# A third shared group of a mixture of experts ahead of its expert stage, in halves between other TensorE work

## The reference

```
x = x + attention(layernorm(x))                    # cumulative K^T V state per head
h = layernorm(x)
scores = softmax(h @ Wg); weights, indices = top_k(scores, 4)
for e in range(32):                                # at most CAP = 2048 pairs per expert
    y[tok] += (silu(h[tok] @ W1[e]) * (h[tok] @ W3[e]) @ W2[e]) * weight
z = silu(h @ Ws1) * (h @ Ws3) @ Ws2                # the shared expert, 256 wide inside
out = x + y + z
```

## Time and profile before

| | us |
|---|---|
| three timed runs, median | 640.11 (639.14 to 641.84) |
| the profiled execution | 639.03 |
| its span, first to last instruction | 637.3 |
| TensorE busy (products) | 581.1 (91%) |
| VectorE busy | 365.5 (57%) |
| ScalarE busy | 393.3 (62%) |
| GpSimd busy | 375.0 (59%) |
| mean granted TensorE clock | 0.973 of full |

### The profile page before, as it was taken

The page is one execution under the profiler, slowest core; times in us unless marked ns, Lnnn a source line. Parts: engine busy times, 40 slices in busy tenths (PEclk is TensorE's granted clock), DMA queues, the critical chain, the costliest instruction groups (busy, mean ns, idle before and its releaser), DMA issues.

```text
span 637.3 us, 16757 instructions
## 1 busy us (share of the span) xinstructions
PE 581.1 (91%) x4081; PEld 420.9 (66%) x4081; DVE 365.5 (57%) x1420; ACT 393.3 (62%) x1306; POOL 375.0 (59%) x425
## 2 busy tenths in 40 slices
PE   4799999999999977699899999999999999997981
PEld 1466766666676654268668888888888888554551
DVE  4589999999999995433223233322333223248686
ACT  2589988989898973216656766676666766410100
POOL 4124778787788786605445555565665555497360
PEclk9999999999999997699999999999999999998995
DMA  8994444444444547957776655565565555397773
GB/s 275 303 291 167 175 169 179 178 161 169 187 161 169 200 185 231 348 173 226 235 224 190 184 181 184 181 186 182 182 182 185 187 180 181 113 412 251 228 264 132
DMA packets 70154, 130.53 MB, mean 205 GB/s; under 512 B 10288, under 2 KB 48560, under 8 KB 70064
## 3 DMA queue, kind: packets, MB, share of 16 engines
q1 hardware_dynamic: 52128, 83.32, 41.1%
q0 software_dynamic: 13824, 41.96, 17.8%
q10 hardware_dynamic: 4112, 4.19, 2.0%
HBM read 61.11 MB, written 68.32 MB: 203 GB/s over the span
## 4 chain that ended last, share of the span: by engine, by line
PE 65%; POOL 10%; issue 8%; DVE 8%; SPq 4%; ACT 3%; DMA 2%; DVEq 0%; ACTq 0%; POOLq 0%
PE pS L730 19%; PE pS L742 9%; PE pS L554 8%; POOL xs L369 6%; PE pQV L659 4%; PE pS L590 3%; POOL w L387 3%; PE pT L723 2%; PE pO L676 2%; PE pQV L723 2%; PE pQV L568 2%; PE pO L568 2%; PE pO L642 1%; DVE xall L994 1%; PE pT L631 1%
## 5 line engine op out<-in xcount | busy, mean ns | idle before, releaser
L398 POOL DMA_INDIRECT ys<-gsh,dst x160 | 152.9, 956 | 131.9 <-ACT gsh L531 130.0
L730 PE MATMUL pS<-w,after_a 128*128 x640 | 165.8, 382 | 0.2 <-ACT after_a L520 0.2
L369 POOL DMA_INDIRECT xs<-xg,posi x128 | 124.3, 971 | 49.6 <-issue 25.6
L730 PEld LDWEIGHTS pS<-w,after_a 128*128 128x128 f32 x640 | 109.1, 190 | 9.8 <-issue 0.6
L742 PE MATMUL pS<-w,after_a 128*128 x320 | 95.6, 381 | 0.0
L1008 DVE COPY after_a<-pO 128x128 f32<-128x128 f32 x80 | 23.3, 292 | 93.0 <-PE pO L737 92.0
L1008 DVE COPY after_a<-pT 128x128 f32<-128x128 f32 x80 | 23.3, 292 | 92.8 <-PE pT L737 91.4
L531 ACT ACTIVATE gsh<-pS,xg 128x256 f32<-128x256 f32 x160 | 75.9, 474 | 0.4 <-issue 0.4
L530 ACT CAST dst<-xg 128x1 int32 x160 | 30.6, 191 | 60.9 <-PE pS L742 60.9
L659 PE MATMUL pQV<-w 128*128 128x512 f32 x128 | 64.0, 624 | 0.5 <-ACT w L464 0.5
L554 PE MATMUL pS<-x2T_all,ws 128*128 128x512 f32 x128 | 62.1, 640 | 2.4 <-DVE gsh L978 1.4
(11 more groups left out here) (157 smaller groups left out, 1105.8 us busy)
## 6 DMA issues: line engine op xcount, KB each, us to landing
xg<-xs SPq DMA_DIRECT2D x160, 160.0 KB, 2.2
ys<-gsh SPq DMA_DIRECT2D x32, 512.0 KB
w<-ys SPq DMA_DIRECT2D x32, 512.0 KB, 6.2
xs<-padrow SPq DMA_DIRECT2D x33, 160.0 KB, 2.4
w<-in_L_ffn_W ACTq DMA_DIRECT2D x1, 4096.0 KB, 21.9
out<-xall SPq DMA_DIRECT2D x32, 128.0 KB, 1.8
xall<-in_L_attn_X SPq DMA_DIRECT2D x1, 3072.0 KB, 14.0
ys<-gsh,dst POOLq DMA_INDIRECT x160, 2.7
```

What stands on the lines that cost most here:

```text
L369: pool.indirect_dma_start(out=xs, out_offset=bass.IndirectOffsetOnAxis(ap=posi[:, a.r8, k:k + 1], axis=0), in_=xr[:, a.r8, :], in_offset=N ...
L398: pool.indirect_dma_start(out=ys, out_offset=bass.IndirectOffsetOnAxis(ap=dst[:, j % 8:j % 8 + 1], axis=0), in_=y[:, j % 8, :], in_offset= ...
L730: last = pe.matmul(pS[a.b][:, 0:2 * F], xgT[:, a.b, k, :], w13[:, bass.ds(e, 1), k, :, :].rearrange("p a n f -> p (a n f)"), start=(k == 0 ...
```

## The change

NPRE becomes 3, so that groups 0, 1 and 2 stand before the experts and 3 to 7 behind them. Eight of the twelve halves go into other banks than `pS[2m+n]`, those that the attention or the table leave free at the time. The halves are issued one at a time between other work: (1,0,0) ahead of tile 27's ranks, (0,0,0) after the last attention output, (0,0,1) and (0,1,0) after the logits of tiles 29 and 30, (0,1,1) between the last transposes and the last logits, (1,0,1) after these, and (1,1,0), (1,1,1), (2,0,0), (2,0,1) after the counts. The row products of the table write into pT0 alone. VectorE does three gates in the middle of the table's chain and the gate of (1,1) behind it, and the last two halves of group 2 stand between the output products.

```
+        early = {(1, 0, 0): pQV, (1, 0, 1): pO, (1, 1, 0): pT1, (1, 1, 1): pS[0], (2, 0, 0): pS[2], (2, 0, 1): pS[1],
+                 (2, 1, 0): pS[3], (2, 1, 1): pT1}
+
+        def h_bank(g, m, n):
+            return early.get((g, m, n), pS[2 * m + n])
-        NPRE = 2
+        NPRE = 3
...
             def shared_half(g, m, n):
-                wait(pe, S["gsh_done"], FC * (g - 1) + m + 1)
                 for k in range(KC):
-                    last = pe.matmul(pS[2 * m + n][:], ws13[:, k, n, m * P:(m + 1) * P],
+                    last = pe.matmul(h_bank(g, m, n)[:], ws13[:, k, n, m * P:(m + 1) * P],
                                      x2T_all[:, k, g * TG:(g + 1) * TG], start=(k == 0), stop=(k == KC - 1))
...
                 if (a := tile_of(6)) is not None:
+                    if a.t == NT - 5:
+                        pe.wait_ge(S["ws_in"], 48)
+                        pe.wait_ge(S["v_done"], NT)
+                        shared_half(1, 0, 0)
...
-            shared_half(0, 1, 1)
+            shared_half(1, 1, 0)
+            pe.wait_ge(S["silu_done"], 1)
+            shared_half(1, 1, 1)
+            pe.wait_ge(S["silu_done"], 2)
+            shared_half(2, 0, 0)
+            pe.wait_ge(S["gsh_done"], 1)
+            shared_half(2, 0, 1)
             pe.wait_ge(S["tab_blk"], 1)
...
-            for g in range(1, NPRE):
-                for m in range(FC):
-                    shared_h(g, m)
-                shared_z(g - 1)
-            shared_z(NPRE - 1)
+            pe.wait_ge(S["gsh_done"], 3)
+            shared_z(0)
+            shared_half(2, 1, 0)
+            shared_z(1)
+            shared_half(2, 1, 1)
+            shared_z(2)
...
+            def half_gate(g, m):
+                wait(dve, S["silu_done"], FC * g + m + 1)
+                wait(dve, S["z_ps"], QT * (g - 1))
+                dve.tensor_tensor(gsh[:, g % 2, m, :], sg[:, m, :], h_bank(g, m, 1)[:], ALU.mult).then_inc(S["gsh_done"], 1)
...
             tab(dve.tensor_tensor_scan(endt[:], ones_f[:], ntf[:], 0.0, ALU.mult, ALU.add))
+            dve.wait_ge(S["ys_zeroed"], 16 * ZC)
+            half_gate(0, 0)
+            half_gate(0, 1)
+            half_gate(1, 0)
...
-            dve.wait_ge(S["ys_zeroed"], 16 * ZC)
-            for g in range(NPRE):
-                shared_gate(g)
-                if g > 0:
-                    shared_add(g - 1)
-            shared_add(NPRE - 1)
+            half_gate(1, 1)
+            shared_add(0)
+            half_gate(2, 0)
+            shared_add(1)
+            half_gate(2, 1)
+            shared_add(2)
```

More of the change, by code:

```diff
@@ L507, in shared_silu @@
                     wait(act, S["gsh_done"], FC * (g - 1) + m + 1)
-                    act.activation(sg[:, m, :], pS[2 * m][:], ACT.Silu).then_inc(S["silu_done"], 1)
+                    act.activation(sg[:, m, :], h_bank(g, m, 0)[:], ACT.Silu).then_inc(S["silu_done"], 1)
             for g in range(NPRE):
@@ L633, in step @@
                     last.then_inc(S["logits_ps"], 1)
+                    if a.t == NT - 3:
+                        shared_half(0, 0, 1)
+                    if a.t == NT - 2:
+                        shared_half(0, 1, 0)
                     if a.t == NT - 1:
-                        shared_half(0, 1, 0)
+                        pe.wait_ge(S["x2_done"], NT)
+                        shared_half(1, 0, 1)
                 if (a := tile_of(2)) is not None:
@@ L685, in _ @@
             pe.matmul(pT0[:, 0:E], ones16[:], mcum[:, NT % 2, :], start=True, stop=True).then_inc(S["cnt_ps"], 1)
[L687 removed]
             pe.wait_ge(S["x2T_done"], NT)
[L689 removed]
             pe.wait_ge(S["state_done"], NT)
[L692 removed]
+            shared_half(1, 1, 0)
[5 more added lines that the diff above has]
+            shared_half(2, 0, 1)
             pe.wait_ge(S["tab_blk"], 1)
             for n in range(2):
[L695 removed]
+                pe.matmul(pT0[0:1, D + n * P:D + (n + 1) * P], ejc[:, n:n + 1], ident[:], start=True, stop=True)
             for n in range(2):
@@ L936, in _, with shared_gate, shared_add, parts_add @@
             pipelined(NT, 7, step)
+            def half_gate(g, m):
+                wait(dve, S["silu_done"], FC * g + m + 1)
+                wait(dve, S["z_ps"], QT * (g - 1))
+                dve.tensor_tensor(gsh[:, g % 2, m, :], sg[:, m, :], h_bank(g, m, 1)[:], ALU.mult).then_inc(S["gsh_done"], 1)
+            def shared_gate(g):
+                for m in range(FC):
+                    half_gate(g, m)
+            def shared_add(g):
+                for q in range(QT):
+                    t = g * QT + q
+                    wait(dve, S["z_ps"], t + 1)
+                    dve.tensor_tensor(xall[:, t, :], xall[:, t, :], (pQV, pO)[q % 2][:, 0:D], ALU.add).then_inc(S["z_done"], 1)
+            def parts_add(g):
+                for t in range(g * QT, (g + 1) * QT):
+                    wait(dve, S["parts_sum"], t + 1)
+                    dve.tensor_tensor(parts[:, t % PB, 0, :], parts[:, t % PB, 0, :], parts[:, t % PB, 1, :], ALU.add
+                                      ).then_inc(S["half_sum"], 1)
+                for t in range(g * QT, (g + 1) * QT):
+                    wait(dve, S["z_done"], t + 1)
+                    wait(dve, S["half_sum"], t + 1)
+                    dve.tensor_tensor(xall[:, t, :], xall[:, t, :], parts[:, t % PB, 0, :], ALU.add).then_inc(S["summed"], 1)
             r = [0]
@@ L971, in _ @@
             dve.tensor_copy(brow[:], pT0[0:1, 0:256]).then_inc(S["brow_done"], 1)
-            dve.tensor_copy(erow[:], pT1[0:1, 0:256]).then_inc(S["erow_done"], 1)
-            def shared_gate(g):
-                for m in range(FC):
-                    wait(dve, S["silu_done"], FC * g + m + 1)
-                    wait(dve, S["z_ps"], QT * (g - 1))
-                    dve.tensor_tensor(gsh[:, g % 2, m, :], sg[:, m, :], pS[2 * m + 1][:], ALU.mult).then_inc(S["gsh_done"], 1)
-            def shared_add(g):
-                for q in range(QT):
-                    t = g * QT + q
-                    wait(dve, S["z_ps"], t + 1)
-                    dve.tensor_tensor(xall[:, t, :], xall[:, t, :], (pQV, pO)[q % 2][:, 0:D], ALU.add).then_inc(S["z_done"], 1)
-            def parts_add(g):
-                for t in range(g * QT, (g + 1) * QT):
-                    wait(dve, S["parts_sum"], t + 1)
-                    dve.tensor_tensor(parts[:, t % PB, 0, :], parts[:, t % PB, 0, :], parts[:, t % PB, 1, :], ALU.add
-                                      ).then_inc(S["half_sum"], 1)
-                for t in range(g * QT, (g + 1) * QT):
-                    wait(dve, S["z_done"], t + 1)
-                    wait(dve, S["half_sum"], t + 1)
-                    dve.tensor_tensor(xall[:, t, :], xall[:, t, :], parts[:, t % PB, 0, :], ALU.add).then_inc(S["summed"], 1)
-            dve.wait_ge(S["ys_zeroed"], 16 * ZC)
-            for g in range(NPRE):
-                shared_gate(g)
-                if g > 0:
-                    shared_add(g - 1)
-            shared_add(NPRE - 1)
+            dve.tensor_copy(erow[:], pT0[0:1, 256:512]).then_inc(S["erow_done"], 1)
+            half_gate(1, 1)
[4 more added lines that the diff above has]
+            shared_add(2)
             def expert_step(tile_of):
```

9 lines of the change are left out of this document (4 added, 5 removed).

## The result

| | before | changed |
|---|---|---|
| median, us | 639.71 (639.14 to 641.84, 4 runs) | 631.37 (630.08 to 632.47, 4 runs) |
| profiled execution | 639.03 | 631.95 |
| its span | 637.3 | 630.2 |

A forecast was written before the change was run, and what follows sets the result against it. SyncE's pads and loads were taken to bound the first fifty microseconds of the experts, VectorE the end. Span 637.3 - 4.1 - 0.1 = 633.1, 634.8 with what lies around it, 635.9 as median; range 633.6 to 638.6.

The forecast's parts named there:

- "Up to 612.77 ... I move nothing": End stage until the fourth quarter of parts is added: same TensorE and VectorE work in the same order, no gain.
- One group less, "-4.1 us": End stage: one shared group fewer lets VectorE end at 630.4 instead of 634.6, -4.1 us, bounds -5.5 to -3.
- the lock reading: End stage: a VectorE add with both inputs in SBUF, met by a GpSimd add, waits for the whole of it.
- Rival D: End stage: the whole slot is saved, fourth and fifth parts groups moving up; -8, 632; chance 0.07.
- The clock at 249 to 255: Stage between attention and experts: TensorE's granted clock is 1.0 from 245 to 265, where 0.50 stood from 250.
- rival A: Before the experts: the clock still falls at 249, experts start at 283.6, median 637.1; chance 0.13.
- Count product done at 255.9: Before the experts: at full clock the count product is done at 255.9, before 257.35.
- Experts' start at 280.3: Third group ahead of the experts: first expert product at 280.3, 2.2 us ahead of 282.52; gain cut to 0.1 us.
- Rival B: Table stage: the clock falls and stays down, experts start at 286.9, +4.3, time 640.3; chance 0.08.
- "If they start later by x, all of x is lost": Experts' start, coupled to SyncE's loads: starting earlier gains at most 0.2 us, starting later loses the whole delay.

The follow-up runs named there:

- f_before: Kernel before with 16 one-column products (64 TensorE instructions) added at its start, moving the instruction fetch; 682.85 us, ratio 0.992.
- f_after: Changed kernel with 48 one-column products (192 TensorE instructions) added at its start, moving the instruction fetch; 680.49 us, ratio 0.990.
- y_before: Kernel before with GpSimd waiting at four places until VectorE is through with a parts group; 678.65 us, ratio 0.986.
- tail_only: Kernel before with the last shared group left out of the end and put nowhere; 682.74 us, ratio 0.997.
- y_after2: Changed kernel with GpSimd waiting at four places until VectorE is through with a parts group, second run; 627.56 us, ratio 0.978.
- early_two2: Kernel before, still two groups ahead of the experts, but their halves placed as the change does; second run, 638.52 us, ratio 0.998.
- a_third: Changed kernel unchanged, measured a third time; 630.39 us, ratio 0.985 to the kernel before on the same chip.
- y2_after: As y_after2, and VectorE instead of GpSimd makes the first sums of the last four tiles; 626.05 us, ratio 0.976.
- b_again: Kernel before unchanged, measured and profiled again on another chip; 689.56 us (one run).

## Why the prediction was right or wrong

*"Up to 612.77 ... I move nothing": the step that failed.* The same work in the same order moved by 3.6 us (62.3 to 58.7 behind the experts), since VectorE's part of it depends on where GpSimd pauses, GpSimd on one load, and the load on a fetch that TensorE's instruction count places. f_before and f_after move this stretch by the fetch alone (59.2 with six groups, 63.3 with five), and y_before moves it by pauses alone (53.7). I had read that stretch as a fixed schedule, though the 4.90 and 5.70 us for four adds of 0.36 stood in the trace, and a wait of 3.88 us of TensorE hung on them.

*One group less, "-4.1 us": mis-sized.* With the fetch left where it was it measures -1.7 and -2.3 (f_after's 84.8 and tail_only's 84.2 against 86.5; only tail_only is of the same chip as the 86.5), outside my bounds of -5.5 to -3. I had let GpSimd's last adds stay at 621.04 (70.5 behind the experts). They come later, at about 74.5 in f_after, as GpSimd and the loads wait for freed tiles, and so the fifth parts group is held until 73 and not 71.8, and the sixth falls under them in part, ending at 76.7. (Two slips of arithmetic change nothing: 634.6 less 630.4 is 4.2, and by its own terms the forecast's range is 634.5 to 637.0.) That GpSimd's hold-up and not TensorE's slot sets the gain was right there, and the lock reading with it: four adds of VectorE against a stream take 5.7 us, without it 1.42. The Trainium skill (SBUF — State Buffer, § SBUF: two separate sides) calls the shared port pair an exclusive lock; y_after2 agrees, with eight adds in 3.5 us that took 10.5 against GpSimd's stream.

How the -6.75 measured (86.80 to 80.05) is shared out depends on the order, for the two act together. First the group, then the fetch: some -2 and -4.8 (84.8 to 80.05). First the fetch, then the group: -1.4 (86.5 to 85.1) and -5.1. What doesn't depend on it is the place: -3.6 up to the fourth parts group, where I had nothing, and -3.15 behind it, where I had -4.1. The two errors have opposite signs. Had the fetch stayed where it was, the time would have lain above my forecast, near 637 (639.7 less 2.0 and the 0.35 of the experts' end).

*Rival D* had the right size (632, "the fourth and fifth parts groups to move up") for the wrong reason: not because a TensorE slot is saved; in tail_only and f_after the slot is gone and the fourth parts group doesn't move up (63.0 and 63.3). That it landed on the measured time is luck.

*The clock at 249 to 255: right.* It is 1.00; rival A is out. The forecast of 1.0 up to 265 failed behind that, with 0.71 between 255 and 260.

*Count product done at 255.9: off by 1.3, and the sum itself held.* In early_two2, with the same list up to there, it starts at 255.70 and is done at 255.88. In the changed kernel it starts at 257.02: a dip at 232.8 costs 0.54 us at the spot and 1.3 at the counts. The profile of the changed kernel and those of a_third, y_after2 and y2_after have the dip, early_two2 doesn't. Why stays open; no run was aimed at it.

*Experts' start at 280.3: wrong, 283.82.* Of 3.5 us, 1.3 is that dip; 1.8 is the half (1,1,0), which I priced at full clock and which ran at half of it, behind rank steps of 0.18 us with holes of up to 1.6 between them; the stretch behind the row products, 16.4 us in the sum, took 16.9. Rival B had the place but not the size: the low clock ended after one half.

*"If they start later by x, all of x is lost": wrong.* They started 1.3 later and ended 0.35 earlier: loads 8 to 28 took 39.3 us instead of 40.9. What I had taken for SyncE's own pace, 1.96 us a tile, isn't fixed. That an earlier start gains little here held in the time (early_two2, 5.8 us earlier, ratio 0.998), but its experts end 2.65 us earlier, where I had allowed 0.2.

## What to carry to other kernels

When VectorE and GpSimd both add within SBUF, look for eight adds that take three times their length, and put waits into GpSimd's list where VectorE has a deadline: here that took 5.8 us off the end stage, where the change's own idea alone took 1.7 to 2.3, and the two together 12.4 (86.5 to 74.15). Treat no stretch as fixed because its lists are unchanged; ask which one event late or early would reorder two engines that share a port. And before crediting a gain to an edit that changes the count of instructions, pad the old kernel by as many idle ones: here that alone moved the time by 0.8%. Then look in which stage it did, for most of it lay elsewhere than where the fetch was at work.

## What the runs showed of the hardware that I had not expected

Instruction fetches share the DMA engines with data: 39 packets on q8 and 51 on q14 in the changed kernel's profile, 0.64 and 0.42 MB. One packet of 16 KB in a burst at 406 GB/s took 1.03 us and goes with one sixteenth of a load 1.2 us late, a slowest load of 16.4 instead of 15.4 us and a pause of GpSimd of 0.61 us. GpSimd in a gapless stream lets one add of VectorE in per add of its own (5.70 us for four, 1.42 alone). TensorE's clock fell to 0.71 on average between 255 and 260 though its longest hole was 1.6 us and it had been at 1.00 for the ten before. And chips differ by 7% on one kernel (640.88 and 686.95 us), all of it ahead of the experts' end (550.50 and 601.31). Gaps of up to 1.2 us between small dependent instructions of VectorE are a part of it: the way from the count product to the row products takes 10.4 us in b_again for 4.8. The rest was not followed up.
